# The four forms that add dt's bias, moved behind the bound of the states in chunk 7

## The reference

```python
x = x + attn_a(layernorm(x))   # a selective state space layer
x = x + ffn(layernorm(x))      # a router over 16 experts, 6 taken
x = x + attn_b(layernorm(x))   # linear attention with flow normalisation
x = x + ffn(layernorm(x))      # the same router and experts
```

```python
delta = softplus(x_conv @ dt_proj_w.T + dt_proj_b); delta = clip(delta, 1e-4, 10.0)
# for every t:
dA = exp(clip(dt[..., None] * A, -10.0, 0.0))
h  = dA * h + dt[..., None] * bt[:, None, :] * xt[..., None]
hn = clip(norm(h), 1e-6, None)
h  = where(t % 16 == 15, h * where(hn > 10.0, 10.0 / hn, 1), h)
y  = einsum('bn,ben->be', ct, h) + D_param * xt
# router, for every token:
probs = softmax(logits)   # the 6 largest, normalised to sum 1, weigh the experts' products
```

## Time and profile before

| | |
|---|---|
| median of 3 runs (4530.81 to 4533.28) | 4531.89 us |
| the profiled execution's own time | 4533.19 us |
| its span, first to last instruction | 4531.1 us |
| PE, DVE, ACT, POOL busy | 4257.0, 3634.9, 3057.3, 2587.6 us |
| mean granted TensorE clock, share of full speed | 0.985 |

### The profile page before, as it was taken

How to read it: one execution, slowest core, us unless ns; L and a number is a source line. 1 busy time by engine, 2 the same in 40 slices (tenths; PEclk the granted TensorE clock), 3 DMA queues, 4 the chain that set the end, 5 groups by cost and what they waited for, 6 DMA issues and landing times.

```text
span 4531.1 us, 79942 instructions
## 1 busy us (share of the span) xinstructions
PE 4257.0 (94%) x22592; PEld 2961.4 (65%) x22592; DVE 3634.9 (80%) x9610; ACT 3057.3 (67%) x8912; POOL 2587.6 (57%) x1284
## 2 busy tenths in 40 slices
PE   5899999999999999999999999978999999999999
PEld 4777777777777777777777777644444444444444
DVE  3899999999999999999999999854656657566666
ACT  5888888888888888888888888824332323333321
POOL 3988888888888888888888888820000000000000
PEclk8999999999999999999999999989999999999999
DMA  2111111111111111111111111110000000000000
GB/s 99 59 50 62 49 61 50 57 53 57 54 57 54 57 54 57 54 57 54 57 54 57 54 57 54 55 36 11 6 16 16 6 16 6 16 16 7 6 6 10
DMA packets 91560, 187.49 MB, mean 41 GB/s; under 512 B 16160, under 2 KB 58016, under 8 KB 90912
## 3 DMA queue, kind: packets, MB, share of 16 engines
q1 hardware_dynamic: 90272, 180.78, 12.2%
q10 hardware_dynamic: 1152, 5.14, 0.3%
HBM read 168.05 MB, written 17.83 MB: 41 GB/s over the span
## 4 chain that ended last, share of the span: by engine, by line
PE 61%; DVE 16%; issue 14%; POOL 6%; ACT 2%; DVEq 1%; DMA 0%; POOLq 0%; SPq 0%; ACTq 0%
PE ps L668 28%; PE ps L642 7%; DVE macc L982 5%; PE ps L744 4%; PE ps L721 4%; POOL prod L315 3%; PE ps L788 3%; PE ps L707 2%; PE ps L701 2%; PE ps L761 2%; PE ps L729 2%; POOL hb L323 1%; DVE dtt L1142 1%; PE ps L738 1%; PE ps_dA L788 1%
## 5 line engine op out<-in xcount | busy, mean ns | idle before, releaser
L668 PE MATMUL ps<-w_x,mxT 128*128 128x512 f32 x4096 | 1931.5, 601 | 66.8 <-DVE macc L982 66.8
L982 DVE SCALAR_TENSOR_TENSOR macc<-ps,gate,macc 128x256 f32<-128x256 f32 x2048 | 977.7, 477 | 484.4 <-PE ps L668 402.8
L893 DVE TENSOR_TENSOR_SCAN hb<-ps_dA,hb 128x1088 f32<-128x1088 f32 x512 | 1240.6, 2423 | 105.9 <-POOL hb L323 97.9
L315 POOL TENSOR_TENSOR prod<-hb,cbc 128x1024 f32<-128x1024 f32 x512 | 1122.5, 2192 | 248.9 <-DVE hb L912 232.8
L323 POOL TENSOR_TENSOR hb<-u,bbc 128x1024 f32<-128x1024 f32 x512 | 1201.6, 2347 | 75.1 <-POOL prod L315 71.1
L378 ACT ACTIVATE zr<-dt,aneg 128x128 f32<-128x128 f32 x4096 | 1240.8, 388 | 1.3 <-DVE dt L1031 1.2
L668 PEld LDWEIGHTS ps<-w_x,mxT 128*128 128x128 f32 x4096 | 727.5, 191 | 738.8 <-issue 602.9
L642 PEld LDWEIGHTS ps<-prod,ident 128*128 128x128 f32 x8192 | 946.3, 192 | 151.6 <-POOL prod L315 90.7
L642 PE MATMUL ps<-prod,ident 128*128 128x128 f32 x8192 | 964.2, 276 | 40.3 <-POOL prod L315 40.3
L387 ACT ACTIVATE ps_dA<-zr 128x1024 f32<-128x1024 f32 x512 | 518.5, 1013 | 0.0
L394 ACT ACTIVATE sq<-hb 128x64 f32<-128x64 f32 x512 | 158.0, 309 | 219.6 <-DVE hb L893 217.2
(11 more groups left out here) (193 smaller groups left out, 4851.3 us busy)
## 6 DMA issues: line engine op xcount, KB each, us to landing
bbc<-bcd SPq DMA_DIRECT2D x128, 512.0 KB, 3.8
cbc<-bcd SPq DMA_DIRECT2D x128, 512.0 KB, 3.8
xt<-in_x SPq DMA_DIRECT2D x128, 128.0 KB, 3.6
x2d<-macc SPq DMA_DIRECT2D x64, 128.0 KB, 1.7
out_dram<-macc SPq DMA_DIRECT2D x64, 128.0 KB, 1.7
w_x<-in_w_x ACTq DMA_DIRECT2D x1, 4096.0 KB, 13.1
hb<-x2d SPq DMA_DIRECT2D x32, 128.0 KB, 2.5
sz<-x2d SPq DMA_DIRECT2D x16, 128.0 KB, 2.4
```

The source lines that it names most:

```text
L315: TT(dst, states, cc, ALU.mult).then_inc(M["prodp"], 1)
L668: last = mm(banks[p % len(banks)][:], mxT[k][:, j, :], w_x[:, j, p * 512:(p + 1) * 512], start=(j == 0), stop=(j == KD - 1))
L893: V.tensor_tensor_scan(states, dA, states, 0.0, ALU.mult, ALU.add).then_inc(M["scan"], 1)
L982: STT(macc[k][:], banks[(e // 2) % len(banks)][:, (e % 2) * D:(e % 2 + 1) * D], gate[k][:, e:e + 1], macc[k][:], ALU.mult, ALU.add).then_i ...
```

## The change

On DVE, in chunk 7 of `step`, the block under `if F:` with its two waits (dtp, dt) and its four forms is taken from ahead of the router's last step and put behind `end(7)`, the bound. The instructions and their signals are the same.

```diff
                 start(7)
                 router(9, 10)
                 halfway(7)
+                router(10, 11)
+                if X_:
+                    route_gate(i - 2, k)
+                end(7)
                 if F:
                     v.wait_ge(M["dtp"], AHEAD + i + 3)
                     v.wait_ge(M["dt"], AHEAD + (i + 2 if G_ else 0))
                     for e in range(EB):
                         TS(dtt[:, e, :], F0[:, e * P:(e + 1) * P], b_dt[:, e:e + 1], 40.0, ALU.add, ALU.min)\
                             .then_inc(M["dtb"], 1)
-                router(10, 11)
-                if X_:
-                    route_gate(i - 2, k)
-                end(7)
```

## The result

The changed kernel takes 4580.12 us at the median of 4 runs (4575.93 to 4580.33), the kernel before beside it 4531.61 (4530.81 to 4533.28): ratio 1.0104, 95% interval 1.0091 to 1.0116. That is 48.5 us, about 1%, slower; 4579 was forecast.

The account below looks back on a forecast made before the run. DVE's sequence from chunk 7 to chunk 0's bound was taken to set the period. 42.8 us for 28 loop pairs, 3.7 for four steps outside and 0.6 for two early ones made +47 us: 4579 us, range 4556 to 4594.

Parts of the forecast that it names:

- (1): Chunk 7 on DVE: forms leave a covered place, selp still ends with POOL's instruction, bound and product stay; gain 0.
- (2): Between L912 and scan(0), steps without the loop's branch: the four forms delay the scan by 1.03 us.
- (3): Every second step, ending in the loop's branch: the queued forms hide the branch, so scan(0) comes 0.74 us later.
- (4): Chunk 0: L1031 comes later, finds POOL idle and takes 0.43 instead of 0.67 us; -0.24 us in every second step.
- (6): The sum: 0.79 us in steps without branch, 0.74 with it, 28 pairs making 42.8 us; +47 us in all.
- The row that decides: selp in route_gate, 447 ns in the pipeline against 165: not slow, but blocked until POOL's instruction is over.
- the first rival: Selp issued early is not held to POOL's end, the bound waits for ACT's factor alone: +5 us, 4537; chance 0.07.
- (5): ACT's queue behind the forms: xn ends later, covered by ACT's 1.31 us idle with 0.1 left; cost 0.
- The second: Rival: chunk 7's states come 0.75 us earlier and PE limits, giving 45 us back, 4487 us; chance 0.05.
- The third: Rival: mechanism right but neither cover holds, branch exposed (0.95) and L1031 staying 0.67 (1.03): 4592 us; chance 0.08.

Follow-up runs that it names:

- e1: The changed kernel with the router's rest, selp's second input, in PSUM instead of SBUF in the first phase: 4559.4 us, ratio 1.0056.
- e3: The kernel before with the router's rest in PSUM in the first phase, nothing moved in chunk 7: 4515.4 us, ratio 0.9961.
- e7: The changed kernel with both rest and selp in PSUM in the first phase: 4539.6 us, ratio 1.0015.
- e2: The kernel before with only the router's last step, selp and gate moved ahead of the four forms, bound still last: 4587.5 us, ratio 1.0118.
- e5a: The kernel before with one of the four forms moved behind the bound, three staying ahead of the router's last step: 4534.2 us, ratio 1.0005.
- e4: The kernel before with the bound moved ahead of selp and gate, behind the four forms and the router's last step: 4595.6 us, ratio 1.0139.
- e8: The kernel before with the bound directly behind the four forms, then router's last step, selp, gate; rest and selp in PSUM: 4525.9 us, ratio 0.9986.

## Why the prediction was right

Medians over 20 steps of each kind, in us from the scan of chunk 7:

| | predicted | measured |
|---|---|---|
| (1) bound, no branch | unmoved (5.26 before) | 5.26 |
| (1) product of chunk 7 | unmoved (5.78 before) | 5.77 |
| (2) scan(0) later, no branch | 1.03 | 1.03 (5.61 to 6.64) |
| (3) scan(0) later, with branch | 0.74 | 0.74 (6.06 to 6.80) |
| (4) L1031 | 0.43 in all steps | 0.43 in all steps |
| (4) scan(1) later, no branch, with | 0.79, 0.74 | 0.79, 0.73 |
| (6) a pair of steps | 1.53 | 1.51 (1.49 in the pair shown) |
| first to last scan | 47 | 45.4 |

**The row that decides** was read rightly, and the experiments show it rather than argue it: selp's time is a wait for POOL's instruction (e1, e3, e7), and because of it the bound gains nothing when the forms move away, so that their 1.03 us come in full (e2 has them ahead of the bound and loses no less). Without the hold the changed order stands 8 us behind the kernel before (e7), as the first rival had it, and 24 behind the old order without the hold (e3), which the prediction didn't look at. The step left incomplete is in the same paragraph: I took selp alone for the blocked instruction, though (4) reads L1031, of the same kind as gate, as held. Gate is held as well (e1), which changed nothing in the sum, since gate comes behind selp, but made my number for e1 too low by 14 to 24 us. The Trainium skill's rule on two SBUF inputs, cited there, doesn't cover it; the same section (SBUF — State Buffer, "Who interferes with whom") also names tensor_scalar among the kinds that can contend, under conditions on its operands, and gate's 1.27 us in e1 agree.

**(3)** In the steps with the branch the scan now follows the last form as closely as elsewhere, 1.21 us behind L912 against 1.21. What the branch needs to be hidden is instructions already queued: with one form behind the bound (e5a) scan(0) is at 6.10 against 6.06 before, nearly hidden; behind gate, which waits for selp's result, it is not (0.41 idle in e4 and e8). The queue of 8 that the prediction cites no run tested.

**(5)** ACT's cover held: the squares of scan(0) start at the scan's end, 1593.63 against 1593.60, with the 1.31 us of idle time used up.

**The rivals.** The first was built as e7: predicted +5, measured +8 over its own before (interval 2 to 11). Its two step costs add up to 0.14 a pair; e7's pair takes 91.15 us by the medians against 90.93. The second, PE as the limit, has nothing left: in e7 chunk 7's product comes 0.6 to 0.7 us earlier and the kernel is no faster than before. The third is excluded by (3) and (4).

**How close it is.** The 45.4 us between the scans leave 3 of the 48.5 between the medians. The profiled execution took 4575.93, the other three 4580; its first scan came 2.6 us earlier than before's, a difference in the start-up. What the rest of it is stays open. So the forecast was 1.6 us over what the pipeline lost (47 against 45.4), and that the medians meet it to 1 us is in part luck.

## What to carry to other kernels

When an instruction of 16 elements takes three times its usual time, and always ends a constant 0.03 us behind the end of another engine's, it isn't slow, it is waiting. Look at what ends just before it ends.

When other work is moved out from ahead of such an instruction, the instruction only looks longer and what stands behind it gains nothing, while the work that was moved costs its own time at its new place. Here that was 1.03 us a step. Without the hold the move would still have cost half as much (e7 against e3), because the next wait in line, for ACT's factor, allowed only part of the gain. None of the five other orders of the same instructions beat the kernel before; taking away what blocks did, 18 us for one input in PSUM.

A delay on one engine can cost more than itself: in e4 a fifth of what the pipeline lost, 14 of 65 us, was TensorE at its lower clock.

## What the runs showed of the hardware

- A DVE TENSOR_SCALAR of 128x16 from SBUF to SBUF was held until POOL's TENSOR_TENSOR had ended, 1265 ns at the median of 37 in e1, and 234 ns with its source in PSUM (e7). The 128x1 form just ahead of it (the router's last step, 0.27 us in e1) was not held in the same place.
- The order of issue decides by very little: gate 0.04 us behind POOL's start was held for 2.18 us, 0.15 ahead of it not at all (e4).
- L1031, issued 0.13 us before POOL's instruction ends in the profile, was not lengthened (e5a: 427 ns); issued 0.39 before, it took 0.67 and ended 0.28 behind that end. 0.43 less 0.28 says that POOL lets go some 0.15 us before its end as the profile draws it (an estimate from these two rows).
- The loop's branch cost DVE 0.3 us where it followed the bound (0.47 us from L912 to the scan against 0.17), nothing with the four forms queued (1.21 in both kinds of step), and 0.41 us of idle time behind gate (e4, e8).
- The register instruction of an indexed operand (169 ns) ran behind the wait of its own instruction: the bound came at 4.77 us with it and 4.53 without, both held by the factor (e7, e8).
